# An oscillator step with one increment kept scaled, one identity product replaced by a GpSimd sum, and two scaled copies moved to ScalarE

## The reference

```python
def _derivative(q, p, drive, coupling, bias):
    i_couple = jnp.tanh(q) @ coupling.T
    dq = q - q ** 3 / 3.0 - p + drive + i_couple + bias
    dp = EPSILON * (q + ALPHA - BETA * p)
    return (dq, dp)

dq1, dp1 = _derivative(q, p, ...)
dq2, dp2 = _derivative(q + 0.5 * DT * dq1, p + 0.5 * DT * dp1, ...)
dq3, dp3 = _derivative(q + 0.5 * DT * dq2, p + 0.5 * DT * dp2, ...)
dq4, dp4 = _derivative(q + DT * dq3, p + DT * dp3, ...)
q = clip(q + DT / 6 * (dq1 + 2 * dq2 + 2 * dq3 + dq4)); p = clip(p + ...)   # likewise

gate = silu(bitlinear(x, w_gate)); up = bitlinear(x, w_up)
out = bitlinear(gate * up, w_down)      # int8 activations, ternary weights
```

## Time and profile before

| | |
|---|---|
| median of 3 runs | 595.32 us (595.29 to 595.6) |
| the profiled execution | 597.59 us |
| its span | 595.8 us |
| instructions | 16005 |
| mean granted TensorE clock | 0.996 |
| HBM read, written | 9.78 MB, 4.19 MB |

### The profile page before, as it was taken

How to read it: one execution, slowest core, us unless ns; L and a number is a source line. 1 busy time by engine, 2 the same in 40 slices (tenths; PEclk the granted TensorE clock), 3 DMA queues, 4 the chain that set the end, 5 groups by cost and what they waited for, 6 DMA issues and landing times.

```text
span 595.8 us, 16005 instructions
## 1 busy us (share of the span) xinstructions
PE 573.1 (96%) x6012; PEld 520.6 (87%) x6012; DVE 482.9 (81%) x1330; ACT 399.0 (67%) x980; POOL 253.3 (43%) x400
## 2 busy tenths in 40 slices
PE   9999999999999999999979999999999999999996
PEld 8899999999999988887868888888888888888884
DVE  3777777767677758777689999999999999999996
ACT  3545454454454376685456888888888888888884
POOL 0423323323232145421245555555555555556550
PEclk9999999999999999999899999999999999999999
DMA  8400000000000001500000000000000000000000
GB/s 270 180 2 2 1 1 2 1 1 2 2 1 1 19 3 37 142 21 2 2 1 2 11 19 10 19 19 10 20 19 10 19 19 10 19 20 10 19 27 30
DMA packets 13165, 15.01 MB, mean 25 GB/s; under 512 B 1760, under 2 KB 11296, under 8 KB 13088
## 3 DMA queue, kind: packets, MB, share of 16 engines
q1 hardware_dynamic: 13088, 13.98, 7.3%
HBM read 9.78 MB, written 4.19 MB: 23 GB/s over the span
## 4 chain that ended last, share of the span: by engine, by line
PE 67%; DVE 18%; ACT 6%; issue 5%; DMA 1%; POOL 1%; SPq 1%; DVEq 0%; ACTq 0%
PE PS L492 21%; PE PS L325 17%; PE PS L348 13%; PE PS L551 4%; DVE q_s L1130 4%; PE PS L573 4%; PE PS L466 3%; DVE h_s L1116 2%; PE PS L410 2%; DVE h_s L1103 2%; DVE h_s L1109 2%; DVE PS L1079 2%; ACT k_s L800 2%; PE PS L419 1%; ACT big L730 1%
## 5 line engine op out<-in xcount | busy, mean ns | idle before, releaser
L492 PE MATMUL PS<-k_s,h_s 128*128 128x128 f32 x1024 | 140.1, 280 | 8.9 <-ACT k_s L800 8.3
L492 PEld LDWEIGHTS PS<-k_s,h_s 128*128 128x128 f32 x1024 | 126.1, 191 | 19.7 <-issue 14.5
L325 PE MATMUL PS<-part 128*128 128x256 f32 x900 | 115.6, 286 | 0.0
L325 PEld LDWEIGHTS PS<-part 128*128 128x128 f32 x900 | 109.8, 191 | 0.0
L800 ACT ACTIVATE k_s<-h_s 128x128 f32<-128x128 f32 x256 | 65.2, 301 | 47.3 <-DVE h_s L1109 37.0
L348 PE MATMUL PS<-big,wrk 128*128 128x128 f32 x744 | 88.4, 275 | 2.2 <-DVE big L958 2.2
L348 PEld LDWEIGHTS PS<-big,wrk 128*128 128x128 f32 x744 | 85.8, 192 | 2.8 <-DVE big L958 2.8
L1267 POOL COPY h_s<-big 128x256 f32<-128x256 f32 x32 | 21.4, 670 | 129.0 <-DVE big L958 129.0
L492 PE MATMUL PS<-h_s 128*128 128x128 f32 x384 | 61.6, 283 | 0.4 <-DVE PS L1098 0.4
L689 ACT ACTIVATE big<-big 128x256 f32<-128x256 f32 x32 | 13.3, 416 | 63.9 <-DVE big L940 63.9
L492 PEld LDWEIGHTS PS<-h_s 128*128 128x128 f32 x384 | 50.4, 191 | 3.1 <-DVE PS L1098 0.6
(11 more groups left out here) (188 smaller groups left out, 1198.8 us busy)
## 6 DMA issues: line engine op xcount, KB each, us to landing
out<-q_s SPq DMA_DIRECT2D x32, 128.0 KB, 1.7
x_s<-in_xT SPq DMA_DIRECT2D x14, 256.0 KB, 6.2
k_s<-in_wgT SPq DMA_DIRECT2D x4, 208.0 KB, 2.5
k_s<-in_wuT SPq DMA_DIRECT2D x4, 208.0 KB, 2.7
k_s<-in_wih SPq DMA_DIRECT2D x3, 256.0 KB, 4.5
wrk<-in_whh SPq DMA_DIRECT2D x3, 256.0 KB, 5.1
h_s<-in_wdT SPq DMA_DIRECT2D x3, 256.0 KB, 3.5
x_s<-in_xT SPq DMA_DIRECT2D x4, 128.0 KB, 3.6
```

What stands on the lines that cost most here:

```text
L325: r = pe.matmul(p, y, x, start=i == 0, stop=i == len(passes) - 1)
L492: return pe.matmul(cm(stage_bank(slot), m), w, x, start=False, stop=True, skip_group_check=True)
```

## The change

The increment of q in stage 2 is kept scaled: qs[1] is stored times held[2] = 2 - 2*kap. That is the factor with which id_z3 would have added it (apart from the 1/3 that seed_4 applies), so that the identity product of stage 3 is gone, and dq on GpSimd becomes (qs[0] - q) + qs[1], in place, with a wait for its own first half and for nexts of stage 1. The third identity matrix is not made. The factors of tanh, square, cubic, nexts, t3 and t4 take the new scale. v1 and uz are made on ScalarE (`scaled_p`), behind hf in steps 3 and later, behind stage 0's square in steps 0 to 2. No transfer is changed.

```diff
-    of_ps = (3.0, 3.0, -6.0)
+    held = (1.0, 1.0, 2 - 2 * kap, 1.0)
+    gain = (1.0, held[2], 1.0, 1.0)
+    of_ps = (3.0, 3.0 * held[2], -6.0)
...
-        id_q1, id_s2, id_z3 = (take(128) for _ in range(3))
+        id_q1, id_s2 = (take(128) for _ in range(2))
...
-            pe.wait_ge(s_cp, 4)
+            pe.wait_ge(s_cp, 3)
...
-                linear(4 * t + 3, id_z3, qs[1])
...
                     ac.activation(cm(th[slot % 2], m), cm(src, m), ACT.Tanh,
-                                  scale=(-1 if s == 3 else 1) / lam).then_inc(s_th, 1)
+                                  scale=(-1 if s == 3 else 1) / (lam * held[s])).then_inc(s_th, 1)
...
+            def scaled_p(t):
+                if t:
+                    ac.wait_ge(s_p, t)
+                    ac.wait_ge(s_t1, t)
+                if t < T - 1:
+                    ac.activation(v1, pn[t % 2], ACT.Copy, scale=horner[0]).then_inc(s_v1, 1)
+                if t:
+                    ac.wait_ge(s_WZ, t)
+                ac.activation(uz, pn[t % 2], ACT.Copy, scale=-n3 / lam).then_inc(s_uz, 1)
...
             for t in range(T):
...
                 stage(4 * t)
+                if t < 3:
+                    scaled_p(t)
...
                     ac.activation(hf[:, 0:NI], hN[i % 2], ACT.Identity, scale=h_at(i, 4), bias=mag[:, 0:1]).then_inc(s_hf, 1)
+                    scaled_p(t)
...
             def seed_4(t):
-                ve.wait_ge(s_dq, t + 1)
+                ve.wait_ge(s_dq, 2 * t + 2)
...
-                    for dst, f in ((id_q1, (1 - kap) / 3), (id_s2, -kap / 3), (id_z3, (2 - 2 * kap) / 3)):
+                    for dst, f in ((id_q1, (1 - kap) / 3), (id_s2, -kap / 3)):
...
-            def decayed(t):
-                po_.tensor_scalar(v1, pn[t % 2], horner[0], 0.0, ALU.mult, ALU.add).then_inc(s_v1, 1)
...
-            decayed(0)
...
                     po_.wait_ge(s_t2, t + 1)
-                po_.tensor_scalar(uz, p, -n3 / lam, 0.0, ALU.mult, ALU.add).then_inc(s_uz, 1)
                 po_.wait_ge(s_uz, t + 1)
                 po_.tensor_tensor(two(WZ), two(uz), I_at(t), ALU.add).then_inc(s_WZ, 1)
                 po_.wait_ge(s_next, q_next(t, 0, 1))
                 po_.tensor_tensor(dq, qs[0], q, ALU.subtract).then_inc(s_dq, 1)
+                po_.wait_ge(s_dq, 2 * t + 1)
+                po_.wait_ge(s_next, q_next(t, 1, 1))
+                po_.tensor_tensor(dq, dq, qs[1], ALU.add).then_inc(s_dq, 1)
...
-                    po_.wait_ge(s_p, t + 1)
-                    if t < T - 2:
-                        decayed(t + 1)
```

More of the change, by code:

```diff
@@ L800, in stage @@
                     ac.activation(cm(th[slot % 2], m), cm(src, m), ACT.Tanh,
-                                  scale=(-1 if s == 3 else 1) / lam).then_inc(s_th, 1)
+                                  scale=(-1 if s == 3 else 1) / (lam * held[s])).then_inc(s_th, 1)
                 if slot == 0:
                     ac.wait_ge(s_F, 16)
-                ac.activation(sqP, src, ACT.Square, scale=math.sqrt(cube[s]) / lam).then_inc(s_sq, 1)
+                ac.activation(sqP, src, ACT.Square, scale=math.sqrt(cube[s] * gain[s] / held[s]) / (lam * held[s])).then_inc(s_sq, 1)
+            def scaled_p(t):
[7 more added lines that the diff above has]
+                ac.activation(uz, pn[t % 2], ACT.Copy, scale=-n3 / lam).then_inc(s_uz, 1)
             for t in range(T):
                 stage(4 * t)
+                if t < 3:
+                    scaled_p(t)
                 if t == 0:
@@ L1102, in cubic @@
                 ve.wait_ge(s_sq, slot + 1)
-                ve.scalar_tensor_tensor(w_, sqP, cube[s] * own[s], src, ALU.subtract, ALU.mult).then_inc(s_w, 1)
+                ve.scalar_tensor_tensor(w_, sqP, cube[s] * own[s] * gain[s] / held[s], src, ALU.subtract, ALU.mult).then_inc(s_w, 1)
             def nexts(slot, dst):
@@ L1188, in vector @@
                     ve.wait_ge(s_t2, t + 1)
-                    ve.scalar_tensor_tensor(t3, t2, horner[2], qs[1], ALU.mult, ALU.add).then_inc(s_t3, 1)
+                    ve.scalar_tensor_tensor(t3, t2, horner[2] * held[2], qs[1], ALU.mult, ALU.add).then_inc(s_t3, 1)
                 if t >= 2:
@@ L1195, in vector @@
                     ve.wait_ge(s_next, q_next(t, 2, 1))
-                    ve.scalar_tensor_tensor(t4, t3, horner[3], qs[2], ALU.mult, ALU.subtract).then_inc(s_t4, 1)
+                    ve.scalar_tensor_tensor(t4, t3, horner[3] / held[2], qs[2], ALU.mult, ALU.subtract).then_inc(s_t4, 1)
                 cubic(4 * t + 3, qs[2])
```

## The result

The changed kernel takes 601.75 us (median of 4 runs, 601.35 to 604.69) against 595.31 us before (4 runs, 595.02 to 595.6): a ratio of 1.0117, 95% interval 1.0085 to 1.0149. The forecast was 602.4 us, slower, in a range of 597.0 to 605.2. The profiled execution took 604.69 us for a span of 602.9, 7.1 us more than its counterpart before (597.59 and 595.8).

What follows compares the result with a forecast made beforehand. TensorE and VectorE were both taken as close to full, the tanh limiting the gain. Per step 0.24 - 0.08 + 0.07 = 0.23 us, together +7.1 us on the 595.32 us median: 602.4 us, 8-in-10 range 597.0 to 605.2.

Steps and rivals of the forecast that it cites:

- What bounds the kernel: Oscillator steps: TensorE and VectorE both close to full; removing the 0.55 us identity product gains only 0.08 us a step.
- The second sum: GpSimd's added dq + qs[1], for which seed_4 waits: seed_4 starts at 479.76 instead of 479.52, costing 0.24 us a step.
- The copies: v1 and uz moved from GpSimd to ScalarE behind hf: 0.41 us each, the tanh's slip covered, 0.07 us a step lost.
- The hand-over of v1: ScalarE to GpSimd ahead of t1: t1, L1155, seed_3 and t2 come later, costing 0.07 us a step, between 0 and 0.24.
- The sum: All terms over the 32 oscillator steps: 0.24 - 0.08 + 0.07 = 0.23 us a step, together +7.1 us.
- Steps 0 and 1: First two oscillator steps, where seed_4 already waits for GpSimd: +0.33 us each, less 0.08 in step 1, 0.58 together.
- Step 2: Oscillator step without hf ahead of v1: 0.24 - 0.08 = 0.16 us slower.
- Hiding the sum (1): Rival at seed_4: dq complete by the end of L1177, only the 0.08 gain left, 593.0 us; chance 0.10.
- TensorE as the bound (2): Rival in all 32 steps: the product's 0.55 us comes back each time, -17.6 us, 577.7 us; chance 0.01.
- the draw (3): Rival: v1 in time and the sum ending 0.1 to 0.2 earlier; within 1.2 us of 595.3; chance 0.07.
- the late ScalarE (4): Rival: a copy costs 0.56 and v1 holds t1, L1155 and t2 by 0.24; 11.9 us more, 607.2; chance 0.06.
- The forecast case: Oscillator steps 0.23 us longer, 602.4 us in total; own range 598.5 to 605.0; chance 0.76.

Runs made afterwards that it cites:

- no_sum: The changed kernel with the second GpSimd sum left out, so stage 3 lacks the term of qs[1]: steps of 9.01 us, median 597.31 us.
- uz_only: The kernel before with only uz moved to ScalarE, v1 staying on GpSimd: steps of 8.98 us, median 594.07 us.
- v1_back: The changed kernel with v1 back on GpSimd, uz staying on ScalarE: steps of 9.09 us, median 601.09 us.
- no_sum_v1_back: The changed kernel with the second GpSimd sum left out and v1 back on GpSimd: steps of 8.88 us, median 591.95 us.
- the second four kernels: no_sum and three kernels with cubic of stage 2 issued ahead of seed_4; the kernel before, taken beside them, had a median of 596.2 us.
- run 27: Not a label but a count: the kernel before, unchanged, was run 27 times beside the second four kernels, 593.96 to 599.51 us.

## Why the prediction was right, point by point

- *What bounds the kernel.* Right: taking 0.55 us of work a step off TensorE gave 0.09. The tanh takes over at once, "<-ACT k_s L801", as in step 0 of the kernel before. From nexts of stage 2 to last_next it is 2.05 us; the forecast read 2.06 off that single row. TensorE's gap there is 0.50 us for some 0.6.
- *The second sum.* Forecast +0.24 us; seed_4 stands 0.20 later behind t2, and taking the sum out (no_sum) gives back 0.21. The error is 0.03 in the chain WZ, dq, sum. The sign that was given, VectorE idle for some 0.25 us ahead of seed_4, shows as 0.12 from the end of L1191 (484.03) to seed_4 (484.15); an instruction that need not wait starts 0.08 before the last one's end, so it is 0.20 start to start.
- *The copies.* The duration was right (0.40 for 0.41), and that uz and the tanh's slip are covered too (uz_only, and the tanh, which stands 0.34 us behind the start of nexts for 0.32 before). The hand-over of v1 was mis-sized: forecast +0.07, measured +0.13 to 0.14. I had taken 0.08 from ScalarE to GpSimd and then allowed for less, by analogy to VectorE's 0.08; it is 0.14 (480.20 to 480.34). That v1 holds t1, and t1 the three-element op and t2, held: L1169 ends 0.01 us after t1, and with v1 in its old place or in a better one t2 goes back to 3.50.
- *The sum.* 0.23 us a step forecast, 0.25 measured; 28 steps give 6.9 us for 6.4. That the sum came so near is in part luck: the second sum was put 0.03 too dear and the hand-over 0.06 too cheap, and the two go against each other. Steps 0 and 1 were put at +0.33 and +0.25 and measured +0.2 and +0.1. There GpSimd's ops run beside VectorE's weight work, and the change shifted which of them are stretched by it: in step 0 uz and dq took 0.68 and 1.07 us, WZ, dq and the sum now take 1.01, 0.72 and 0.96. The forecast had added the sum at its undisturbed price. Step 2 was put at +0.16; in the profiled execution the clock's fall covers it, and v1_back, without that fall, shows 10.18 us against 10.03. All these steps together make 7.3 us, and the medians differ by 6.4.
- *Rivals.* Hiding the sum (1) is excluded by seed_4 0.03 us behind its end; TensorE as the bound (2) by no_sum_v1_back; the draw (3) and the late ScalarE (4) by the terms. The forecast case's own range was added up wrongly: 28 x 0.06 + 0.7 is 2.4 us, which makes 597.7 and not 598.5 its lower end, and 0.10 more a step makes 605.2 and not 605.0; the range for 8 in 10 does not hang on it. The forecast of the total, 602.4 us, is 0.65 above the median; the two profiled executions differ by exactly the 7.1 us of the sum, but that is chance in part: 0.5 us more in the steps and 0.3 less in steps 0 and 1, and clock falls of nearly equal price on either side.

## What to carry to other kernels

Work taken off the busiest engine is worth only the distance to the next wait that ends beside it: read that from the instruction that waits for both, in the one place of the trace where the other wait already ends last. When a product is taken out, ask what it had been forcing into order; here the gain lay in letting the seed come later, and two swapped lines turned a loss of 1.2% into a gain of 0.5%. A value moved to another engine costs its place in that engine's list and the hand-over, not its duration.

## What the runs showed of the hardware that was not expected

- ScalarE's hand-over to GpSimd takes 0.14 us (480.20 to 480.34), VectorE's 0.07 (481.82 to 481.89), and GpSimd's to VectorE 0.03 (484.12 to 484.15).
- GpSimd and VectorE hold each other up when VectorE reads two tensors from SBUF, in both directions: t2 0.87 instead of 0.40 and WZ 0.98 instead of 0.73 when they meet. An op of two elements is held until a GpSimd sum ends, 0.43 instead of 0.15, and seed_1 beside v1 takes 0.48 instead of 0.42. The ends show the pattern: the small op ends 0.01 us after the GpSimd op that was running when it started (458.65 and 458.64), and the ones of 256 columns 0.27 to 0.28 after it (t2 at 458.37 and WZ at 458.09, seed_1 at 434.19 and v1 at 433.92).
- TensorE's granted clock falls in some executions for a few us, mostly at two places. In the profiled execution before it was below 1 from 280 to 290 us (0.88 and 0.77 in the two halves), after TensorE had been idle for 0.8 us of the first half; in the changed kernel's from 310 to 315, after it had waited 1.6 us for ScalarE's silu and its table load:

```profile
310.00:315.00 5.00, 4.08 (x18) 3.24 (x18) 2.26 (x8) 2.11 (x7) 1.86 (x3) 0.66 0.00 0
```

  0.66 is the mean of a stretch partly at 1.2 and partly at 2.4 GHz; eight matmuls of step 2 took 1.90 us instead of 1.13. The fall in step 2 costs 1.6 us (11.80 against 10.18 in v1_back), the one ahead of step 0 2 or more: step 0 starts at 292.0 to 294.6 in the five profiles that show it and at 288.4 to 290.9 in the eight that don't. Executions of one kernel spread by it: beside the second four kernels, the kernel before was run 27 times and took 593.96 to 596.46 us at a mean granted clock of 0.998 or more, and 596.89 to 599.51 below it. Whether a fall comes is not settled by the idle time alone, since the kernel before waited 1.6 us at the same place of step 2 and kept its clock.
